# First batch: ternary weights and the halves of q and k ahead of the second scales, stack transfers on one queue

## The reference

```
xn = layernorm(x)                                   # over 256 channels
q, k, v = xn @ Wq, xn @ Wk, xn @ Wv                 # 16 heads of 16
s[l, w] = q[l] . k[l - 63 + w] / 4                  # w = 0 .. 63, -inf before the start
att = softmax(s) @ v_window @ Wo

tern(W) = sign(W) * min(round(|W| / gamma), 1),  gamma = mean|W| + 1e-6
h = gelu(xn @ tern(W_fc).T)                         # 1024 hidden
h = layernorm(h) * ln_w + ln_b
out = x + att + h @ tern(W_proj).T
```

## Time and profile before

| | |
|---|---|
| median of three runs | 396.02 us (395.78 to 396.27) |
| profiled execution | 395.66 us, its span 393.9 us, 13464 instructions |
| busy, share of the span | PE 94%, PEld 68%, DVE 81%, ACT 73%, POOL 59% |
| chain that ended last | PE 85%, DVE 6%, ACT 4% |
| qk_split's upper half on ScalarE | 1023 ns mean |
| stack transfers, issue to landing | q 4.3 us, k 6.3 us (SyncE), median |

### The profile page before, as it was taken

The page is one execution under the profiler, slowest core; times in us unless marked ns, Lnnn a source line. Parts: engine busy times, 40 slices in busy tenths (PEclk is TensorE's granted clock), DMA queues, the critical chain, the costliest instruction groups (busy, mean ns, idle before and its releaser), DMA issues.

```text
span 393.9 us, 13464 instructions
## 1 busy us (share of the span) xinstructions
PE 371.4 (94%) x5798; PEld 266.0 (68%) x5798; DVE 321.0 (81%) x649; ACT 287.5 (73%) x329; POOL 231.7 (59%) x186
## 2 busy tenths in 40 slices
PE   1896899999999999999999999999999999999994
PEld 0344655876588776776587766776677775788873
DVE  3798988599969996899959997799959898998554
ACT  2656168978978698767977698767886698768871
POOL 7901025866685547755575448755576548679871
PEclk9899699999999999999999999999999999999999
DMA  8578029501932087022920177022921176003002
GB/s 283 160 91 95 2 47 165 83 3 33 153 37 52 15 151 109 2 65 46 188 28 27 41 149 109 4 63 46 189 27 30 39 107 100 2 17 81 30 20 78
DMA packets 30684, 29.22 MB, mean 74 GB/s; under 512 B 5664, under 2 KB 29280, under 8 KB 30624
## 3 DMA queue, kind: packets, MB, share of 16 engines
q1 hardware_dynamic: 30048, 27.83, 38.7%
q10 hardware_dynamic: 576, 0.52, 1.3%
HBM read 7.35 MB, written 4.19 MB: 29 GB/s over the span
## 4 chain that ended last, share of the span: by engine, by line
PE 85%; DVE 6%; ACT 4%; DMA 1%; POOL 1%; ACTq 1%; issue 1%; POOLq 1%
PE small L1625 15%; PE big L1564 13%; PE small L1636 10%; PE big L1538 9%; PE big L1615 7%; PE big L1550 6%; PE big L1603 5%; PE big L1578 5%; PE small L1652 5%; PE big L1608 4%; PE big L1584 3%; PE big L1526 2%; PE small L1642 2%; DMA x_in<-in_x 1%; DVE negmax L1026 1%; ACT qk_split L731 1%
## 5 line engine op out<-in xcount | busy, mean ns | idle before, releaser
L578 POOL TENSOR_TENSOR p_parts<-probs,p_parts 128x1024 f16<-128x1024 f32 x64 | 136.3, 2134 | 112.6 <-ACT p_parts L762 112.6
L761 ACT ACTIVATE probs<-big,exp_scale 128x1024 f32<-128x1024 f32 x64 | 71.5, 1117 | 22.8 <-PE big L1608 20.7
L1026 DVE TENSOR_REDUCE negmax<-big 128x8 f32<-128x1024 f32 x64 | 77.5, 1222 | 4.8 <-PE big L1584 3.4
L762 ACT ACTIVATE p_parts<-big,exp_scale 128x1024 f16<-128x1024 f32 x64 | 71.4, 1115 | 0.0
L1625 PE MATMUL small<-proj_t,g_hi 128*128 128x256 f16 x256 | 57.7, 273 | 0.0
L1625 PE MATMUL small<-proj_t,g_lo 128*128 128x256 f16 x256 | 57.5, 272 | 0.0
L776 ACT ACTIVATE g_hi<-big,lnw_s 128x512 f16<-128x512 f32 x64 | 39.8, 690 | 16.4 <-PE big L1615 16.4
L1564 PE MATMUL big<-fc_t,xt_hi 128*128 128x512 f16 x128 | 48.5, 379 | 2.2 <-ACT gel L749 1.2
L1564 PE MATMUL big<-fc_t,xt_lo 128*128 128x512 f16 x128 | 48.5, 379 | 0.0
L1020 DVE SCALAR_TENSOR_TENSOR g_lo<-big,lnw_s,g_hi 128x512 f16<-128x512 f32 x64 | 46.5, 745 | 1.7 <-ACT g_hi L776 1.3
L1062 DVE SCALAR_TENSOR_TENSOR y_bufs<-small,rs,res 128x256 f32<-128x256 f32 x32 | 15.5, 483 | 29.9 <-PE small L1625 26.8
(11 more groups left out here) (133 smaller groups left out, 810.0 us busy)
## 6 DMA issues: line engine op xcount, KB each, us to landing
q_stack<-qk_split SPq DMA_DIRECT2D x48, 128.0 KB, 4.3
k_stack<-qk_split SPq DMA_DIRECT2D x44, 128.0 KB, 6.3
x_in<-in_x SPq DMA_DIRECT2D x8, 512.0 KB, 5.7
out<-y_bufs SPq DMA_DIRECT2D x32, 128.0 KB, 2.8
v_odd<-v_even SPq DMA_DIRECT2D x16, 132.0 KB, 2.5
v_odd<-v_even SPq DMA_DIRECT2D x16, 99.0 KB, 2.2
gel<-in_w_fc SPq DMA_DIRECT2D x1, 1024.0 KB, 6.5
y_bufs<-in_w_proj SPq DMA_DIRECT2D x1, 1024.0 KB, 8.3
```

What stands on the lines that cost most here:

```text
L578: g.tensor_tensor(p_lo[:, (b * NJ + j) % PB], probs[:, (b * NJ + j) % PB], p_hi[:, (b * NJ + j) % PB], ALU.subtract).then_inc(*sig(p_lo_re ...
L761: s.activation(probs[:, (b * NJ + j) % PB].rearrange("p i (u q) -> p u i q", u=2), st, ACT.Exp, scale=exp_scale[:, 0:1]).then_inc(*sig(exp ...
L762: s.activation(p_hi[:, (b * NJ + j) % PB].rearrange("p i (u q) -> p u i q", u=2), st, ACT.Exp, scale=exp_scale[:, 0:1]).then_inc(*sig(p_hi ...
L1026: v.tensor_reduce(negmax[:, :, j], slot[b, "sa", j][:].rearrange("p a (u k) -> p (a u) k", k=P), AX.X, ALU.max, negate=True).then_inc(*sig ...
```

## The change

All edits are in batch 0:

- TensorE: spread 1 moves from behind qk 0 to behind fc 1, and the second warm job has eight matmuls in place of five.
- VectorE: ternary(0) comes directly behind thresholds(0), then both lower halves of qk, and only then `largest(1)`, `scales(1)`, thresholds(1) and weight_lower(1).
- ScalarE: the scaling of w_v and w_o (`weight_upper(1)`) moves from between the two upper halves of qk to behind the second gelu; `load_upper_keys` is gone.
- SyncE: `load_stack(0, 1, 0)` issues k's upper half, between q's lower half and k's lower half.

```diff
--- before.py
+++ after.py
@@ -264,8 +264,8 @@
 
 
         FIRST = [(0, "wmax", 0), (0, "spread", 0), (0, "warm", 0), (0, "xt", 0), (0, "sums", 0), (0, "wmax", 1),
-                 (0, "warm", 1), (0, "qk", 0), (0, "spread", 1), (0, "sums", 1), (0, "qk", 1), (0, "fc", 0),
-                 (0, "fc", 1), (0, "fc", 2), (0, "fc", 3), (0, "v", 0), (0, "crow", 0), (0, "sa", 0), (0, "sa", 1),
+                 (0, "warm", 1), (0, "qk", 0), (0, "sums", 1), (0, "qk", 1), (0, "fc", 0), (0, "fc", 1), (0, "spread", 1),
+                 (0, "fc", 2), (0, "fc", 3), (0, "v", 0), (0, "crow", 0), (0, "sa", 0), (0, "sa", 1),
                  (0, "sa", 2), (0, "sa", 3), (0, "sa", 4), (1, "xt", 0), (0, "sa", 5), (0, "sa", 6), (0, "csum", 0),
                  (0, "sa", 7), (0, "gt", 0), (1, "qk", 0), (0, "mt", 0), (0, "gt", 1), (1, "qk", 1), (0, "gt", 2),
                  (0, "gt", 3), (0, "st", 0), (1, "fc", 0), (0, "proj", 0), (1, "fc", 1), (1, "fc", 2), (1, "fc", 3),
@@ -422,6 +422,7 @@
             load_x(1)
             load_stack(0, 0, 0)
             load_stack(0, 0, 1)
+            load_stack(0, 1, 0)
             load_stack(0, 1, 1)
             shift_values(0, 0)
             load_maxima(0)
@@ -789,26 +790,16 @@
                 s.activation(scratch[:].rearrange("p a n -> p (a n)"), raw.rearrange("p k n -> p (k n)"), ACT.Abs,
                              accum_out=red[:, 5 + i:6 + i]).then_inc(abs_ready, 1)
 
-            def load_upper_keys():
-
-                act.wait_ge(stacks_filled, 1)
-                act.wait_ge(*at(0, qk_hi_ready, 2))
-                for half in range(2):
-                    for product in (0, 2):
-                        r = half * W + product * DH
-                        s.dma_start(k_stack[r:r + DH, 0, :, W:], qk_split[:, 1, half, 0]).then_inc(*sig(stacks_loaded[0]))
-
             normalize(0)
             absolute(0)
             weight_upper(0)
             xt_upper(0)
             absolute(1)
             qk_upper(0, 0)
-            weight_upper(1)
             qk_upper(0, 1)
-            load_upper_keys()
             gelu(0, 0)
             gelu(0, 1)
+            weight_upper(1)
             gelu(0, 2)
             gelu(0, 3)
             v_upper(0)
@@ -1179,13 +1170,13 @@
             weight_lower(0)
             xt_lower(0)
             thresholds(0)
+            ternary(0)
+            qk_lower(0, 0)
+            qk_lower(0, 1)
             largest(1)
-            ternary(0)
             scales(1)
-            qk_lower(0, 0)
             thresholds(1)
             weight_lower(1)
-            qk_lower(0, 1)
             split_norm()
             ternary(1)
             hidden_statistics(0, 0)
@@ -1506,7 +1497,7 @@
             gt = (g_hi, g_lo)
             cts = (ct_hi, ct_lo)
             ps_hl = (p_hi, p_lo)
-            WARM = (3, 5)
+            WARM = (3, 8)
 
             def job(b, kind, n):
                 if kind != "warm":
```

## The result

| | before | changed |
|---|---|---|
| median, 19 runs each | 395.99 us (395.06 to 396.31) | 395.03 us (394.72 to 396.32) |
| ratio | | 0.9983, 95% interval 0.9976 to 0.9990 |
| the same again, 8 runs (before: 23) | 395.59 us | 395.33 us, ratio 0.9991 (0.9980 to 1.0003) |
| profiled execution, span | 395.66, 393.9 | 396.32, 394.5 |

By the medians the gain is 0.96 us in the first comparison and 0.26 in the second; by the ratios it is 0.7 and 0.4 us, 0.1 to 0.2%, and the second interval takes in no change.

A forecast was written before the change was run, and what follows sets the result against it. TensorE bounds the kernel, but VectorE's fixed order sets batch 0's start-up. The removed 1.42 wait and lock stall are replaced by waits of 0.26, 1.6, 1.05 and 0.2: net 0.0, 396.0 us, range 394.9 to 397.5.

The forecast's parts named there:

- The method: Batch 0 start-up: follow VectorE's new order to v_even's lower half, now at 35.67; bringing v forward wins at most 1.42 us.
- The number: Whole kernel: net change 0.0, so 395.7 us for the profiled execution and 396.0 on the median's scale; chance 0.48.
- The stall: VectorE's 2.13 us diag, held by GpSimd's memset, goes; p_parts starts at 16.52, at the short memset's release.
- Lost lock: Rival, VectorE start-up: p_parts waits to 18.61 as diag did, v's lower half 0.55 late; 396.3 us, chance 0.20.
- Part 1: TensorE's warm job, five to eight matmuls: 0.65 more inside the pause costs nothing; clock holds, qk 1 ends at 21.68.
- Parts 2 and 3: VectorE's new order: waits of 0.26 and 1.6 for qk halves, 1.05 for spread behind fc 1; v's lower half 35.65.
- Part 4: TensorE's fc and v: v's upper half ready at 32.6, was 35.64; hidden, since VectorE comes 3.0 later.
- Part 5: Twelve transfers on SyncE: ScalarE loses 2.73 us of issues; last issued by about 26, landing near 35.4; worth nothing.
- The falling clock: Rival, TensorE at qk 0: clock drops despite eight warm matmuls, scaled at 27.18, 1.7 late; 397.7 us, chance 0.14.
- The old chain: Rival: VectorE's waits are shorter, so v's upper half 3.0 us earlier counts; 393.0 to 395 us, chance 0.10.
- The slow stretch: Rival: TensorE's low-clock period after 40 us falls and rises elsewhere, -0.5 to -2; about 394.8 us, chance 0.08.

The follow-up runs named there:

- the queue edit alone: Kernel before, with SyncE issuing all twelve stack transfers, k's upper half included, and ScalarE none: 394.12 us, ratio 0.9958.
- the scales in the waits: Changed kernel with all second-scale work in VectorE's two waits for qk_split, spread 1 before fc 0, weight_upper(1) before the first gelu: 393.12 us, 0.9934.
- the queue edit undone: Changed kernel with ScalarE again issuing k's upper half in place of SyncE: 397.50 us, ratio 1.0050 against before.
- early second scales: Changed kernel with largest(1) between the two lower halves, spread 1 between qk 1 and fc 0, weight_upper(1) ahead of gelu 1: 393.78 us, 0.9950.
- six warm matmuls: Changed kernel with six warm matmuls in place of eight and two unread ones behind crow: 395.14 us, ratio 0.9987.
- the two kernels built on before: Kernel before with eight warm matmuls (395.08 us), and before with three unread matmuls behind crow (395.17 us); both 0.9991.
- the clock held: Changed kernel with all second-scale work in VectorE's waits for qk_split, six warm matmuls and sixteen unread ones behind crow: 392.26 us, 0.9914.
- run 11: Not a label of a run: the sentence says that in a run, 11 to 15 of SyncE's 206 to 210 issues take over 0.7 us.

## Why the prediction was right

*The method* (walk VectorE's order; TensorE and ScalarE supply only waits) was right as long as the stacks were in time. Where v_even moved by a us or more and they were, the last exponentials moved with it to 0.1 us. Against before: -1.5 and -1.5 with the queue edit alone, +2.4 and +2.3 with it undone in the changed kernel, +1.5 and +1.5 with five warm matmuls. With the scales in the waits it moved on without the transposes.

*The number* came out partly by luck. The prediction left out two things of opposite sign: in both profiles the start-up is 0.5 to 0.7 worse than forecast, and the end of the program is 0.5 better.

*The stall* (early start of p_parts): right in all profiles of the changed order. P_parts, waiting, went at the release each time. "Lost lock" did not happen, though v_even came at its 36.2, for another reason. The Trainium skill's "SBUF — State Buffer", section "SBUF: two separate sides", gives the lock to whoever starts first and does not speak of a release; here p_parts had waited from 16.46, and the large memset that came next, recorded from 16.72, took 2.99 in place of 2.02. No row shown has both engines waiting at a release.

*Part 1* is the term that was mis-sized. Three more warm matmuls were costed at 0.65, inside the pause. That took their rate from the one profile in which they ran 0.2155 apart. In both profiles of the changed kernel they run 0.43 apart, so eight end at 17.0 and push qk 0 by 0.7. So in these profiles the costed 1.89 for eight became 3.62, and there was no pause through which the clock could hold. Where eight ran as fast as costed or nearly so (1.89 with the queue edit undone, 2.63 with early second scales), nothing is pushed, and qk 0, at 16.05 and 16.08, runs at the full clock as forecast. The second profile of before shows that its five are no steadier: 2.34 against 1.24.

*Parts 2 and 3*: 1.50 for the forecast 1.6, 1.05 for 1.05. The net of 0.0 came out as +0.7 and +0.5 in the two profiles; in the first 0.15 of it is there before the changed code begins (xt_lo ends at 16.11 against 15.96), the rest is from part 1, which also shows as the unforecast wait of 0.68 and 0.63 at the first lower half.

*Part 4* was right: v's upper half was ready about 3 us ahead of VectorE (33.30 against 36.19 in the second profile).

*Part 5* has SyncE issue the last of the twelve by about 26. Its issues took 0.64 each and the last ended at 28.55, of which only 0.75 is the late qk 0. The stacks were in at 36.60 and 36.46, when sa 0 starts, and not near 35.4 (35.53 with six warm matmuls and qk 0 on time); that cost nothing here, but it is the term that bound with the scales in the waits. Part 5 also says "worth nothing either way". That holds for the transfers, whose rate is the same on one queue as on two, and is wrong for the edit: ScalarE's 2.7 us of issues stood ahead of the table load, and taking them away is worth 1.6 us by itself. The walk had used it without naming it; w_hi at 26.85 could not have come so early otherwise.

*Where the measured gain comes from* the prediction did not see. It took the end of the program as fixed. About 0.5 us is saved by SyncE's last issue, no longer beside an instruction fetch, and three matmuls that nobody reads bring the same at both places in TensorE's stream that were tried. In the changed kernel's second profile the last exponentials start 0.57 later than in before and the end comes 0.50 sooner behind them. That this is most of the change's gain is inferred from that and from the two kernels built on before, both at 0.9991; that it is all of it is not shown (0.9983 and 0.9991 for the changed one, with intervals that overlap, and no profile of one of its executions near 395).

*The rivals.* The falling clock did not come in the six profiles with eight warm matmuls; with five it came in three of five. In the changed kernel with five its sum for scaled, 27.18, met 27.07, and its time, 397.7, was a us too high (396.65). The old chain did not carry its gain. The slow stretch moved (it began near 37.5 in both profiles and ended at 44.4 and at 47.6), in the second profile without any gain; what it can give was seen with the scales in the waits and with the clock held, 0.9 us from the transposes on.

Open: which executions start with slow warm matmuls, and which of SyncE's issues is caught by a packet on q8. Of the 206 to 210 in a run 11 to 15 take over 0.7 us, all but at most one of them beside such a packet; in before 13 of the 15 end 0.35 to 0.42 after a packet's end, the last one among them. About as many others, 11 to 16 a run, also touch a packet and are not slow. The first profile's 0.89 us wait in batch 1 followed one of the slow ones, falling on the maxima and not on v_odd as in the second; whether that explains other long executions was not tried.

## What to carry to other kernels

When an edit frees an engine, price it alone: here the queue edit brought 1.6 us, and a reordering made with it spent that in three new waits of the engine that sets the pace. Work whose operands are ready belongs into that engine's waits: doing so with the second scales turned the same edits into 2.8 us, and 3.5 with the clock held. When a gain of 0.1% comes without any shift at the place that was edited, compare the end of the program too: here it was the last store.

## What the runs showed of the hardware

- The granted clock reads 1.00 from the start of the span, but the eight warm matmuls there ran 0.43 apart (3.62 us). Ahead of its first change the column doesn't tell the level; the matmuls' steps do.
- A GpSimd memset and a VectorE tensor_scalar (128x2048, SBUF to SBUF) exclude each other: 2.02 us became 2.99, 0.32 became 1.28, and a 3x3 operation took 2.13. In the profiles shown a waiting VectorE went at the release. Not every VectorE instruction is held: fc_t, which reads two tiles, took its 2.35 (17.78 to 20.13) while the large memset ran to 19.71.
- A DMA issue on SyncE, 0.33 us for a store, took 0.75 to 1.15 in the three profiles in which a 16 KB instruction packet was under way beside it, and ended 0.38 after it.
- Stack transfers moved 117 GB/s on one queue as on two (window 24.5 to 35.5).
- Eight transposes of fp32 128x128 blocks took 1.97 us at a granted clock of 0.50 and 1.09 at the full one.
